# The first block of a random-feature attention kernel: the clamp of phi's angles on GpSimd instead of VectorE

## What is computed

```python
def _rfs(xw, ab, AB, gs):
    dot_products = jnp.einsum('...d,rd->...r', xw, ab[:, None] * gs)
    correction = (0.5 * jnp.sum(xw * xw, axis=-1))[..., None] * (ab * ab)
    return 1.0 / math.sqrt(NUM_RFS) * AB * jnp.exp(dot_products - correction)

weights = _rfs(input_weights, ab, AB, proj_matrix)          # attention
feats = _rfs(x, ab, AB, proj_matrix)
attn = jnp.einsum('bsr,or->bso', feats, weights)

real = jnp.einsum('bti,io->bto', x, jnp.cos(theta + theta_noise))   # second layer
imag = jnp.einsum('bti,io->bto', x, jnp.sin(phi + phi_noise))
ffn = jnp.sqrt(real * real + imag * imag)

x = _layernorm(x + attn(x))
x = _layernorm(x + ffn(x))
```

## Time and profile before

| | |
|---|---|
| median of 3 timed runs | 704.66 us (704.25 to 705.13) |
| the profiled execution's own time | 704.95 us |
| span of that execution | 703.1 us |
| mean granted TensorE clock | 0.992 |
| stretch in which phi's angles are reduced on DVE | 59.4 to 68.4 us |

### The profile page before, as it was taken

The page is one execution under the profiler, slowest core; times in us unless marked ns, Lnnn a source line. Parts: engine busy times, 40 slices in busy tenths (PEclk is TensorE's granted clock), DMA queues, the critical chain, the costliest instruction groups (busy, mean ns, idle before and its releaser), DMA issues.

```text
span 703.1 us, 10329 instructions
## 1 busy us (share of the span) xinstructions
PE 686.5 (98%) x3024; PEld 564.6 (80%) x3024; DVE 600.3 (85%) x967; ACT 448.7 (64%) x658; POOL 227.5 (32%) x271
## 2 busy tenths in 40 slices
PE   8999899999999999999999999999999999999993
PEld 7877688888888888888888888888888888888872
DVE  5789899888898988889888888999888898888785
ACT  7746867466675848567584855758485675746443
POOL 5663564504114050503205050230405032050406
PEclk9999999999999999999999999999999999999997
DMA  8862012272746538074553808355380835544001
GB/s 302 236 136 60 16 60 90 70 209 82 157 149 128 179 75 233 21 182 132 119 179 76 237 15 201 113 119 179 86 228 15 208 105 121 177 99 96 29 31 60
DMA packets 168785, 88.08 MB, mean 125 GB/s; under 512 B 112576, under 2 KB 139200, under 8 KB 168768
## 3 DMA queue, kind: packets, MB, share of 16 engines
q1 hardware_dynamic: 167616, 85.77, 45.0%
q0 software_dynamic: 1152, 2.10, 1.8%
HBM read 57.41 MB, written 30.44 MB: 125 GB/s over the span
## 4 chain that ended last, share of the span: by engine, by line
PE 90%; DVE 6%; ACT 2%; POOL 1%; issue 1%; POOLq 0%; DVEq 0%
PE token_ps L894 8%; PE token_ps L896 8%; PE token_ps L895 8%; PE token_ps L1002 6%; PE token_ps L1003 6%; PE token_ps L1004 6%; PE project_ps L844 4%; PE project_ps L843 4%; PE project_ps L842 4%; PE turn_ps L843 4%; PE turn_ps L844 4%; PE turn_ps L842 4%; PE project_ps L1003 3%; PE project_ps L1002 3%; PE project_ps L1004 3%; PE turn_ps L1003 3%
## 5 line engine op out<-in xcount | busy, mean ns | idle before, releaser
L462 POOL TENSOR_TENSOR late<-late 128x1024 f32<-128x1024 f32 x29 | 76.2, 2628 | 273.6 <-ACT late L761 273.6
L894 PE MATMUL token_ps<-W_hi,F_hi 128*128 128x512 f32 x256 | 101.1, 395 | 1.8 <-DVE F_lo L1156 1.8
L896 PE MATMUL token_ps<-W_hi,F_lo 128*128 128x512 f32 x256 | 100.3, 392 | 0.0
L895 PE MATMUL token_ps<-W_lo,F_hi 128*128 128x512 f32 x256 | 100.1, 391 | 0.0
L652 ACT ACTIVATE late<-late 128x1024 f32<-128x1024 f32 x29 | 30.8, 1062 | 81.4 <-POOL late L462 81.4
L658 ACT ACTIVATE o_tile<-late,shift,rstd 128x512 f32<-128x512 f32 x58 | 44.1, 809 | 55.8 <-POOL shift L479 55.8
L1002 PE MATMUL token_ps<-T_hi,zT_hi 128*128 128x512 f32 x168 | 65.5, 390 | 0.5 <-DVE zT_lo L1156 0.5
L570 ACT ACTIVATE F_hi<-expo,ab 128x512 fp32r<-128x512 f32 x62 | 44.6, 720 | 32.9 <-DVE expo L1161 32.7
L1003 PE MATMUL token_ps<-T_lo,zT_hi 128*128 128x512 f32 x168 | 65.4, 389 | 0.0
L1004 PE MATMUL token_ps<-T_hi,zT_lo 128*128 128x512 f32 x168 | 65.4, 389 | 0.0
L761 ACT ACTIVATE late<-late 128x1024 f32<-128x1024 f32 x54 | 55.3, 1056 | 14.1 <-DVE late L1571 11.8
(11 more groups left out here) (254 smaller groups left out, 1787.3 us busy)
## 6 DMA issues: line engine op xcount, KB each, us to landing
x_tok<-in_x SPq DMA_DIRECT2D x16, 1024.0 KB, 5.9
out_tokens<-o_tile SPq DMA_DIRECT2D x62, 256.0 KB, 2.6
plain_xT_lo<-in_xT SPq DMA_DIRECT2D x14, 1024.0 KB, 8.3
turned_pair<-late SPq DMA_DIRECT2D x104, 128.0 KB, 2.9
plain_zT_lo<-turned_pair SPq DMA_DIRECT2D x26, 256.0 KB, 2.8
plain_zT_lo<-turned_pair SPq DMA_DIRECT2D x52, 128.0 KB, 2.9
norm_bc<-token_norms SPq DMA_DIRECT2D x15, 256.0 KB, 3.1
plain_T_hi<-in_gsT SPq DMA_DIRECT2D x4, 256.0 KB, 4.5
```

What stands on the lines that cost most here:

```text
L462: pool.tensor_tensor(parts[:, p, :, 0, :], parts[:, p, :, 0, :], parts[:, p, :, 1, :], ALU.add).then_inc(sum_made, 2)
L894: nc.tensor.matmul(o, F_hi[:, c, cols], W_hi[:, c, :], start=(c == 0), stop=False)
L895: nc.tensor.matmul(o, F_hi[:, c, cols], W_lo[:, c, :], start=False, stop=False)
L896: return nc.tensor.matmul(o, F_lo[:, c, cols], W_hi[:, c, :], start=False, stop=(c == C - 1))
```

## The change

Of `reduce_angle`, phi now does only the addition and the multiply-add on DVE and returns. The clamp of each phi chunk is issued on POOL, as `clamp_phi`, behind the turns of phi and ahead of `sum_chunks`. It waits for the multiply-add of its chunk (`angle_step`), and signals a semaphore of its own, `phi_angle_made`, for which ACT's sines of phi wait in place of `angle_made`. Theta's clamps stay on DVE, and their count on `angle_made` is as before.

```diff
-        angle_step, angle_made = sem("angle_step"), sem("angle_made")
+        angle_step, angle_made, phi_angle_made = sem("angle_step"), sem("angle_made"), sem("phi_angle_made")
...
             for c in range(C):
                 count_turns(phi_angle, phi_turns, c, C, 0.0)
+
+            def clamp_phi(c):
+
+                pool.wait_ge(angle_step, C + 2 * (c + 1))
+                pool.tensor_scalar(phi_angle[:, c, :], phi_angle[:, c, :], PI_INSIDE, -PI_INSIDE, ALU.min, ALU.max).then_inc(phi_angle_made, 1)
+
+            for c in range(C):
+                clamp_phi(c)
             sum_chunks(0, theta_turns)
             sum_chunks(1, phi_turns)
...
-            def sine(angles, raw, c, hi, n):
-
-                act.wait_ge(angle_made, n + c + 1)
+            def sine(angles, raw, c, hi, made):
+
+                act.wait_ge(made, c + 1)
...
-                sine(theta_angle, theta_turns, c, cos_hi[:, c, :], 0)
+                sine(theta_angle, theta_turns, c, cos_hi[:, c, :], angle_made)
...
-                    sine(phi_angle, phi_turns, c, sine_chunk(c, True), C)
+                    sine(phi_angle, phi_turns, c, sine_chunk(c, True), phi_angle_made)
...
                 steps += 1
+                if n:
+
+                    return
                 dve.wait_ge(angle_step, steps)
                 ts(angles[:, c, :], angles[:, c, :], PI_INSIDE, -PI_INSIDE, ALU.min, ALU.max).then_inc(angle_made, 1)
```

## The result

The changed kernel takes 705.93 us (median of 14 runs, 704.92 to 706.49), the kernel before 704.52 us in the same rounds (14 runs, 703.41 to 705.50). The ratio is 1.0020, with a 95% interval from 1.0013 to 1.0027: slower by 1.4 us, at the edge of what I had called no change. The forecast was 705.3 and the range 703.4 to 706.6. A repetition in later rounds gave 1.0015 (1.0006 to 1.0024).

The account below looks back on a forecast made before the run. TensorE bounds the kernel, and phi's clamps lie on the chain to the mix. GpSimd and DVE taking turns makes the last sine 0.6 us late: 704.66 + 0.6 = 705.3 us, range 703.4 to 706.6.

Parts of the forecast that it names:

- no change: Whole kernel: a time within 0.2%, or 1.4 us, of the kernel before; given 0.76.
- The turns: Phi part: GpSimd clamps and DVE instructions reading two SBUF tensors lock each other out; last sine 0.6 us late.
- The circle: One phi chunk through DVE, GpSimd and ScalarE: 1.23 + 1.16 = 2.39 us, the same as before.
- The bare clamp: One phi clamp on GpSimd, undisturbed: 0.62 us, taken from another two-operation tensor_scalar of the same shape.
- the clamps really leave DVE: Rival, phi part: GpSimd and DVE don't hinder each other, last sine 1.0 us early, 703.6 us; chance 0.13.
- the dear clamp: Rival, phi part: a GpSimd clamp costs 1.27 instead of 0.62, 2.6 us more, 707.9 us; chance 0.11.
- What is handed on: From phi's last sine to the mix: everything shifts as a whole, the mix from 79.41 to about 80.0.
- The sum's end: Behind the mix of block 1: a matmul stream with no slack, so the 0.6 us reaches the end, giving 705.3.
- after the mix nothing absorbs: From the mix to the end: PE waits only 1.8 us and 0.5 us once each, so a shift stays whole.
- The clock: PE's low clock around the mix, about 1.7 us: rivals gone, 703.6 us, chance 0.10; twice as long, 707.0, chance 0.05.
- a sign of being wrong: After the mix: the prediction is wrong if, among other signs, the low clock stretch vanishes or doubles.

Follow-up runs that it names:

- the moved exponent: Changed kernel with DVE's exponent of feature 2 moved between the last phi chunk's multiply-add and the next lower part; 705.15 us, one execution.
- the four tiny instructions: Changed kernel plus four 128x1 DVE instructions where DVE waits for the first feature; 705.89 us, ratio 1.0013. Also added to other kernels.
- the later sum: GpSimd's second sum of chunks waits for all F_lo; on the changed kernel 704.73 us, ratio 1.0001; on the kernel before 703.77 us, ratio 0.9992.
- the double clamp: Changed kernel with each of phi's clamps done twice on GpSimd; 707.88 us, ratio 1.0039.

## Why the prediction was right, and what it missed

**The turns (right, term by term).** The first clamp was to end 1.16 after the lower part's start: 62.30 - 61.14 = 1.16. The addition was to take 1.09: 1.09 to 1.10. The circle was to be 2.39: 2.38. The last sine was to be 0.6 late: 10.82 against 10.22 after the first addition, 0.60. The bare clamp was to cost 0.62: 0.61 in two experiments. The rival in which the clamps really leave DVE falls with the profile after and with the moved exponent, the dear clamp with the bare 0.61.

**What is handed on (right).** The mix starts 1.0 later than in the first profile, of which 0.43 stood already ahead of phi (DVE's first addition at 59.82 in place of 59.39) and differs from execution to execution; in the repetition PE's lag goes from 0.12 ahead of phi to 0.73 at the mix, 0.6. In the first profile PE's products with phi's third chunk come 0.5 earlier than where the lag stood ahead of phi, and the last ones 0.5 later, as the prediction had it. The slopes of the experiments agree in sign and size: -1.8 local gave -2.3 to -2.5, +2.0 local gave +1.8, the last clamp moved back gave all of the 0.6 and 0.2 to 0.5 more.

**The sum's end (a term was missing).** The forecast took the stream behind the mix as rigid, on the two waits of the earlier trace rows. It isn't: in block 2 a second chain (ScalarE's roots, GpSimd's residual, DVE's statistics and transposes, the DMA round trips through DRAM, DVE's lower parts) runs close behind PE, and in the changed kernel it is the chain that ended last. So the step that failed is "after the mix nothing absorbs": nothing does, but something adds, and the sum had put it at nothing. Compare like with like. The first profile of the kernel before and the second of the changed one both have the low stretch of the clock: PE's lag grew by 0.6 up to the mix and by 0.67 between 143 and 170 us. The second profile of the kernel before and the first of the changed one both lack it: 0.6 and 1.3. The kernel before lost nothing in block 2 in either.

What lies in this second part is seen in pieces, and they overlap with what slack the chain had. DVE's idle stretch gives 0.36 us of spacing; the four tiny instructions take it away. The second DMA round trip, from the start of DVE's transpose to the first use, takes 12.2 and 12.3 us in the two profiles of the changed kernel and 11.5 and 11.7 in those of the kernel before. Over all profiles it is 12.2 to 12.5 in six of the eight kernels with clamps on GpSimd (11.2 and 11.7 in the others) and 11.3 to 11.9 in all six without. And where the low stretch is absent, the first residual of block 2 stands 0.5 us further behind PE in each of the four kernels with clamps on GpSimd and the sum where it was, and not in the kernel before or in the one without a clamp. Why the round trip is longer and the residual later is not shown, and stays open. The padding alone doesn't settle how much the idle stretch costs: with it the lag grew by nothing in one profile, by 1.1 and 0.6 with the later sum, and the kernel with the last clamp on DVE, which has no idle stretch either, lost 1.2 us in block 2; the moved exponent lost 0.8 and the double clamp 1.3.

So of the 1.4 us measured (0.9 to 1.9 by its interval) 0.6 is the predicted term, shown by experiment, and the rest belongs to block 2, shown as a place, with its causes known in part.

**The clock (not settled by the forecast).** The low stretch came in some executions of both kernels and in others not. Its price, 1.6 us in the pair of profiles of the kernel before, was put rightly (1.7), but the change doesn't switch it. In the changed kernel's own first profile it was missing, which the prediction had named as a sign of being wrong; the end was no earlier, because block 2 lost 1.3 us in that execution. In the 64 executions of the six kernels in whose profile PE's wait before the mix is 1.4 us or less, no mean clock of 0.992 or less appears.

**Which side.** I had given 0.16 to slower by over 0.2% and 0.76 to no change; the median lies at 1.0020, between the two. Right in kind, small by half. That 705.93 still lies inside the range is in part luck: its upper end, 706.6, had been set for a dearer clamp, and the clamp was not dearer.

## What to carry to other kernels

An idle GpSimd is no free place for a DVE instruction when DVE's neighbours read two SBUF tensors: the two take turns, and work that is moved comes back as waiting, so put such work beside DVE instructions that read PSUM (here 0.61 us in place of 1.03). Of a chain that loops through three engines, count where its last link ends: with the last clamp back on DVE the other three cost nothing that could be measured. Before costing an edit by the main engine's waits alone, look for a second chain that runs close behind it, compare the chain that ended last stage by stage, and when a stall is removed, name what is late next.

## What the runs showed of the hardware

- DVE with two SBUF inputs and a GpSimd instruction that reads SBUF take turns, in both directions: clamp 1.03 us against 0.61, addition 1.09 against 0.68. Beside a DVE instruction with one SBUF and one PSUM input the clamp took 0.61.
- A minimum and a maximum in one GpSimd instruction cost what multiply and add cost: 0.61 us for 128x512 in f32.
- Four DVE instructions less, some 65 us upstream, put 0.36 us of idle time into the first pass of a loop; four tiny instructions, which start 0.06 us apart, took it away again.
- The same kernel, profiled twice, ran with and without a low stretch of TensorE's clock after the same gap of 1.8 us: spans of 703.1 and 701.5 us.
